# Another order for the scan and for the passage behind it, and a gate mix on VectorE, in a gated recurrent layer with a feed-forward layer

## The reference

```python
u = x @ W_in + b_in
g = sigmoid(x @ W_gate + b_gate)
def step(h_prev, (u_t, g_t, x_t)):
    h_t = tanh(h_prev @ A + u_t @ Bm)
    y_t = h_t @ C.T + u_t @ D.T
    y_t = g_t * y_t + (1.0 - g_t) * x_t        # the gate mix
ys = scan(step, h0 = 0)
x1 = layernorm(x + (ys @ W_out + b_out + x))
h = gelu(x1 @ binarize(w1).T + b1)             # 1024 hidden features
out = layernorm(x1 + h @ binarize(w2).T + b2)
```

## Time and profile before

| | us |
|---|---|
| median of 3 runs (lowest, highest) | 444.82 (444.19, 445.14) |
| the profiled execution | 445.74 |
| its span | 443.9 |
| PE busy | 416.0 (94% of the span) |
| DVE busy | 365.7 (82%) |
| ACT busy | 321.9 (73%) |
| POOL busy | 304.9 (69%) |

### The profile page before, as it was taken

One profiled execution on the slowest core, in us unless ns is written; L12 is line 12 of the kernel. 1 busy time (PEld: TensorE's weight loads), 2 busy tenths in 40 slices (PEclk: granted clock), 3 DMA queues, 4 the chain that ended last, 5 costly groups with the idle time before them and its releaser, 6 DMA issues.

```text
span 443.9 us, 7765 instructions
## 1 busy us (share of the span) xinstructions
PE 416.0 (94%) x2699; PEld 309.2 (70%) x2699; DVE 365.7 (82%) x778; ACT 321.9 (73%) x604; POOL 304.9 (69%) x322
## 2 busy tenths in 40 slices
PE   7999999988876999999999999999999999999882
PEld 5899887876733676776767767677676776766651
DVE  2787778856054889999999999999999999998584
ACT  1346765645264769798898988989889899797791
POOL 6465663253349896977979779797797977683523
PEclk9999999999896999999999999999999999999998
DMA  7954360001010112124241442313423134231222
GB/s 223 362 170 120 121 141 1 0 1 35 15 49 0 49 47 49 48 49 120 71 96 50 95 124 67 96 54 90 128 63 96 63 81 133 58 97 45 52 96 95
DMA packets 43896, 37.19 MB, mean 84 GB/s; under 512 B 35504, under 2 KB 37296, under 8 KB 43856
## 3 DMA queue, kind: packets, MB, share of 16 engines
q1 hardware_dynamic: 42528, 35.66, 28.1%
q0 software_dynamic: 272, 0.66, 0.5%
q10 hardware_dynamic: 1056, 0.36, 0.3%
HBM read 19.90 MB, written 8.39 MB: 64 GB/s over the span
## 4 chain that ended last, share of the span: by engine, by line
PE 58%; DVE 24%; POOL 6%; issue 5%; ACT 5%; ACTq 0%; POOLq 0%; DVEq 0%
PE bank L1089 16%; PE bank L1077 14%; PE bank L939 10%; DVE hid L1443 7%; PE bank L907 6%; PE bank L918 3%; ACT hid L700 3%; POOL xg_lo L433 3%; DVE gT L1456 3%; PE bank L856 3%; DVE bank L1428 3%; DVE bank L1449 2%; DVE xT L1188 2%; PE bank L849 2%; DVE gT L1438 2%
## 5 line engine op out<-in xcount | busy, mean ns | idle before, releaser
L1077 PE MATMUL bank<-xT,w1s 128*128 128x512 f16 x512 | 128.6, 384 | 2.4 <-DVE hid L1443 1.7
L1089 PE MATMUL bank<-w2s,hid 128*128 128x256 f16 x1024 | 125.3, 273 | 1.7 <-DVE gT L1456 0.8
L1089 PEld LDWEIGHTS bank<-w2s,hid 128*128 128x128 f16 x1024 | 98.5, 98 | 32.6 <-issue 5.6
L692 ACT ACTIVATE bank<-bank,b_col,alpha 128x512 f32<-128x512 f32 x128 | 96.7, 756 | 22.2 <-PE bank L1077 21.9
L1443 DVE SCALAR_TENSOR_TENSOR hid<-bank,small,hid 128x512 f16<-128x512 f32 x128 | 95.2, 745 | 14.7 <-ACT hid L700 14.7
L700 ACT ACTIVATE hid<-bank,small 128x512 f16<-128x512 f32 x128 | 86.5, 691 | 19.0 <-PE bank L1089 17.8
L1077 PEld LDWEIGHTS bank<-xT,w1s 128*128 128x128 f16 x512 | 46.4, 99 | 49.6 <-DVE hid L1443 6.9
L639 ACT ACTIVATE hu<-bank 64x128 f32<-64x128 f32 x103 | 27.8, 270 | 52.8 <-PE bank L856 50.0
L453 POOL TENSOR_TENSOR ys_lo<-gT,ys_hi 128x512 fp32r<-128x512 f32 x30 | 38.2, 1277 | 24.9 <-ACT ys_hi L665 24.8
L448 POOL TENSOR_TENSOR gT<-gT,xT 128x512 f32<-128x512 f32 x30 | 38.2, 1274 | 13.0 <-DVE gT L1327 12.8
L440 POOL TENSOR_TENSOR hu_lo<-hu,hu_hi 64x512 fp32r<-64x512 f32 x30 | 37.9, 1262 | 13.2 <-ACT hu_hi L687 10.9
(11 more groups left out here) (159 smaller groups left out, 823.7 us busy)
## 6 DMA issues: line engine op xcount, KB each, us to landing
x_load<-in_L_attn_x SPq DMA_DIRECT2D x16, 512.0 KB, 3.4
gT<-in_L_attn_x SPq DMA_DIRECT2D x15, 512.0 KB, 3.8
out_rows<-gT SPq DMA_DIRECT2D x15, 512.0 KB, 3.5
gT<-in_L_ffn_w SPq DMA_DIRECT2D x2, 1024.0 KB, 7.6
gT<-in_L_attn_x SPq DMA_DIRECT2D x4, 128.0 KB, 2.6
out_rows<-gT SPq DMA_DIRECT2D x2, 256.0 KB, 2.0
xT<-gT SPq DMA_TRANSPOSE x28, 3.2
w_gate<-in_L_attn_W_gate ACTq DMA_DIRECT2D x1, 256.0 KB, 6.9
```

What stands on the lines that cost most here:

```text
L692: nc.scalar.activation(bank[which][:, :], bank[which][:, :], ACT.Gelu, bias=b1_col[:, c:c + 1], scale=alpha1[:, c:c + 1]).then_inc(s_gelu, 1)
L1077: done = nc.tensor.matmul(bank[which][:, :], w1s[:, c, k, :], x1T[:, n, :, part, :, k, :], start=(k == 0 and part == 0), stop=(k == KD - 1 ...
L1089: done = nc.tensor.matmul(bank[tile // 2][:, tile % 2 * DM:(tile % 2 + 1) * DM], hid[:, c % 3, part, tile * P:(tile + 1) * P], w2s[:, :, c ...
```

## The change

No operation on data changes but one: the gate mix of blocks 1 and 2. Everything else is the order in which instructions stand, and the waits that follow from it.

1. **Scan.** The transposes of every block come one step earlier (turned_at, and one extra in the opening), and from block 3 on DVE writes x_out of the second half ahead of u_out of the block before. prepare_rows moves from step 80 to step 76 (PREP, its last matmul to step 79). The y products of block 0 move from steps 86 and 90 to 83 and 85 (FIRST_Y). first_y_high (the high part of the states for them) moves on DVE from behind gate_x_hi(11) to just behind the second weight reduction, hu_low(0, 0) and hu_low(0, 1) on POOL from behind gate_x_low(10) to behind gate_x_low(6). gate_x_lo(9) goes behind the splitting of the C/D table; gate_x_hi(13) and gate_x_lo(13) behind block 0's mix.
2. **Passage.** The orders on PE, DVE, ACT and POOL from step 103 to iteration(1) are new. PE takes the flag's matmul ahead of gate_half(14, 0), and y(1, 0) and y(1, 1) ahead of gate_half(15, 1). ACT's switch to the Gelu table comes later.
3. **Gate mix of blocks 1 and 2.** less_x, then early_gate leaves the product in the bank and early_mix on DVE adds x out of the bank into SBUF; POOL's mix of these blocks is gone, four instructions. The products y(2, 0), y(2, 1), y(3, 0) and hidden(0, 0) now wait for the mix (s_ys), not for the gate alone, since the bank is read by it.
4. **End.** ffn_out(14, 5) stands ahead of hidden(15, 0) and ffn_out(14, 6) ahead of hidden(15, 1); ACT puts the block-12 second norms between the hidden chunks 0 to 3 of block 15; DVE interleaves ffn_scale and second_sum of block 14; the last moments come ahead of a wait.

The diff, cut to its core:

```diff
-    PREP = 10
+    PREP = 9
...
-    FIRST_Y = (WARM + 11 * STEPS + 2, WARM + 12 * STEPS + 2)
+    FIRST_Y = (WARM + 10 * STEPS + 3, WARM + 11 * STEPS + 1)
...
-        return divmod(t + 2 * STEPS, STEPS)
+        return divmod(t + 2 * STEPS + 1, STEPS)
...
-            for place in (6, 8, 10):
-                gate_x_low(place)
-            pool.wait_ge(s_xgl[0], 6)
+            gate_x_low(6)
+            pool.wait_ge(s_xgl[0], 2)
             hu_low(0, 0)
             hu_low(0, 1)
-            gate_x_low(12)
+            for place in (8, 10, 12):
+                gate_x_low(place)
             ys_low(0, 0)
             ys_low(0, 1)
             pool.wait_ge(s_const, 3)
@@ -532,26 +532,20 @@
             add_bias(0)
             pool.wait_ge(s_xb, 1)
             hu_low(1, 0)
+            hu_low(1, 1)
             first_rstd(0, 0)
-            pool.wait_ge(s_rs1, 1)
-            hu_low(1, 1)
             first_rstd(0, 1)
-            mix(1, 0)
-            pool.wait_ge(s_ys, KD + 1)
+            pool.wait_ge(s_rs1, 2)
             hu_low(2, 0)
-            mix(1, 1)
-            pool.wait_ge(s_ys, KD + 2)
             hu_low(2, 1)
+            add_bias(1)
             ys_low(1, 0)
             ys_low(1, 1)
-            add_bias(1)
             residual(0)
-            mix(2, 0)
-            first_rstd(1, 0)
-            pool.wait_ge(s_rs1, 3)
+            pool.wait_ge(s_x1b, 1)
             hu_low(3, 0)
             hu_low(3, 1)
-            mix(2, 1)
+            first_rstd(1, 0)
             first_rstd(1, 1)
             ys_low(2, 0)
             ys_low(2, 1)
@@ -757,22 +751,21 @@
...
-            gate(14, 0)
             act.wait_ge(s_done, 1)
             hu_high(1, 0)
+            gate(14, 0)
             hu_high(1, 1)
             gate(14, 1)
             gate(15, 0)
+            hu_high(2, 0)
+            hu_high(2, 1)
+            x1_hi(0, 0)
+            x1_hi(0, 1)
+            ys_high(1, 0)
             gate(15, 1)
+            ys_high(1, 1)
             nc.scalar.activation(small[0:1, 29:30], ident[0:1, 0:1], ACT.Gelu)
             act.wait_ge(s_scale, 1)
...
-                if n > 1 or (n == 1 and m == 0):
+                if n == 2 and m == 0:
+                    pe.wait_ge(s_ys, KD + 1)
+                elif (n, m) in ((2, 1), (3, 0)):
+                    pe.wait_ge(s_ys, n * KD + m)
+                elif n > 1:
                     pe.wait_ge(s_t, n * KD + m)
...
                     u_whole(2, 1)
+                    transpose_step(*turned_at(t))
...
-                    if o + 2 < NB:
-                        transpose_step(o + 2, s)
+                    if turned_at(t)[0] < NB:
+                        transpose_step(*turned_at(t))
...
                 gate_piece(i)
-            gate_half(14, 0)
             pe.wait_ge(s_cmp, 3)
             nc.tensor.matmul(bank[2][0:1, 0:1], gap_flag, ones[0:NS, 0:1], start=True, stop=True).then_inc(s_cnt, 1)
-            gate_half(14, 1)
+            gate_half(14, 0)
             pe.wait_ge(s_flag, 1)
...
-                    pe.wait_ge(s_t, 2 * KD)
+                    pe.wait_ge(s_ys, 2 * KD)
...
+            gate_half(14, 1)
             gate_half(15, 0)
-            gate_half(15, 1)
             y_products(1, 0)
             y_products(1, 1)
+            gate_half(15, 1)
             x1_transposes(0, 0)
             x1_transposes(0, 1)
             y_products(2, 0)
             pe.wait_ge(s_wt, 32)
             pe.wait_ge(s_scale, 1)
-
-
             hidden(0, 0)
             hidden(0, 1)
+            hidden(0, 2)
             y_products(2, 1)
             out_products(1, 0)
             out_products(1, 1)
-            hidden(0, 2)
+            hidden(0, 3)
             ffn_out(0, 0)
-            hidden(0, 3)
+            hidden(0, 4)
             ffn_out(0, 1)
-            hidden(0, 4)
+            ffn_out(0, 2)
+            hidden(0, 5)
...
+            ffn_out(NB - 2, 5)
             hidden(NB - 1, 0)
-            ffn_out(NB - 2, 5)
+            ffn_out(NB - 2, 6)
             hidden(NB - 1, 1)
-            ffn_out(NB - 2, 6)
...
-            for o in range(2, NB - 1):
-                if o >= WHOLE_U:
-                    u_out(o, 1)
-                    x_out(o + 1, 1)
-                    x_high(o + 1, 1)
+            x_out(4, 0)
+            u_out(3, 0)
+            x_high(4, 0)
+            for o in range(WHOLE_U, NB - 1):
+                x_out(o + 1, 1)
+                u_out(o, 1)
+                x_high(o + 1, 1)
                 if o + 2 < NB:
                     x_out(o + 2, 0)
                 u_out(o + 1, 0)
                 if o + 2 < NB:
                     x_high(o + 2, 0)
...
+
+            def first_y_high(half):
+
+                dve.wait_ge(s_h, 1 + WARM + STEPS)
+                dve.wait_ge(s_sgn, 2)
+                nc.vector.tensor_copy(y0_hu_hi[HALVES[half], :, :], beside(0, half)).then_inc(s_huhi, 1)
+
+            dve.wait_ge(s_prep, 1)
+            first_y_high(0)
+            first_y_high(1)
             gate_x_hi(7)
             gate_x_lo(7)
+            gate_x_hi(8)
...
-            gate_x_lo(9)
-            gate_x_hi(10)
...
-            def first_y_high(half):
-
-                dve.wait_ge(s_h, 1 + WARM + STEPS)
-                dve.wait_ge(s_sgn, 2)
-                nc.vector.tensor_copy(y0_hu_hi[HALVES[half], :, :], beside(0, half)).then_inc(s_huhi, 1)
-
-            gate_x_hi(11)
-            first_y_high(0)
-            first_y_high(1)
-            gate_x_lo(11)
+            gate_x_lo(9)
+            gate_x_hi(10)
...
+            def early_gate(n, m):
+
+                dve.wait_ge(s_yd, n * KD + m + 1)
+                nc.vector.tensor_tensor(y_bank(n, m)[:, :], y_bank(n, m)[:, :], gT[:, n, m, :], ALU.mult).then_inc(s_t, 1)
+
+            def early_mix(n, m):
+                dve.wait_ge(s_t, n * KD + m + 1)
+                nc.vector.tensor_tensor(gT[:, n, m, :], y_bank(n, m)[:, :], xT[:, n, m, :], ALU.add).then_inc(s_ys, 1)
+
...
             first_moments(0, 1)
+            first_norm(0, 0)
             less_x(1, 0)
-            gate_y(1, 0)
-            first_norm(0, 0)
+            less_x(1, 1)
+            early_gate(1, 0)
             first_norm(0, 1)
-            less_x(1, 1)
-            gate_y(1, 1)
+            early_mix(1, 0)
+            early_gate(1, 1)
             x1_lo(0, 0)
+            early_mix(1, 1)
             x1_lo(0, 1)
             less_x(2, 0)
-            gate_y(2, 0)
+            early_gate(2, 0)
...
+            last_moments(1)
             dve.wait_ge(s_last_root, 1)
             nc.vector.scalar_tensor_tensor(out=shift2[:, NB - 1, 0:2], in0=moments[:, 1, 0:2, 0], scalar=-1.0,
                                            in1=rstd2[:, NB - 1, 0:2], op0=ALU.mult, op1=ALU.mult).then_inc(s_last_shift, 1)
-            last_moments(1)
```

More of the change, by code:

```diff
@@ L81, in pieces_at @@
             return 0
-        return 1 if turned_at(t)[0] < NB + 1 and t < NB * STEPS - 7 else 2 if t < NB * STEPS - STEPS else 3
+        return 1 if t < NB * STEPS - 7 else 2 if t < NB * STEPS - STEPS else 3
     def pieces_before(t):
@@ L799, in _ @@
                 hidden_hi(NB - 2, c)
-            for c in range(2):
-                hidden_gelu(NB - 1, c)
-                hidden_hi(NB - 1, c)
+            hidden_gelu(NB - 1, 0)
+            second_norm(NB - 4, 1)
+            hidden_hi(NB - 1, 0)
+            hidden_gelu(NB - 1, 1)
+            second_norm(NB - 4, 2)
+            hidden_hi(NB - 1, 1)
             hidden_gelu(NB - 1, 2)
-            second_norm(NB - 4, 1)
             hidden_hi(NB - 1, 2)
             hidden_gelu(NB - 1, 3)
-            second_norm(NB - 4, 2)
-            hidden_gelu(NB - 1, 4)
+            hidden_hi(NB - 1, 3)
             second_norm(NB - 4, 3)
-            for c in range(3, 5):
-                hidden_hi(NB - 1, c)
-            for c in range(5, HC):
+            for c in range(4, HC):
                 hidden_gelu(NB - 1, c)
@@ L1251, in _ @@
             gate_x_hi(5)
+            gate_x_lo(5)
             u_out(NB - 1, 1)
-            gate_x_lo(5)
             dve.wait_ge(s_w12, 32)
@@ L1270, in _ @@
             nc.vector.memset(ones, 1.0)
-            gate_x_hi(8)
             dve.wait_ge(s_const, 3)
@@ L1317, in _ @@
             nc.vector.tensor_scalar(alpha2_row[:, :], bank[3][:, 0:DM], inv_scale, None, ALU.mult).then_inc(s_prep, 1)
-            gate_x_hi(12)
+            gate_x_hi(11)
+            gate_x_lo(11)
             def less_x(n, m):
@@ L1344, in _ @@
             less_x(0, 0)
+            less_x(0, 1)
+            first_gate(0)
+            first_gate(1)
+            first_mix(0)
+            gate_x_hi(12)
+            first_mix(1)
+            first_high(0)
+            first_high(1)
             gate_x_hi(13)
-            first_gate(0)
             gate_x_lo(13)
-            first_mix(0)
-            less_x(0, 1)
-            first_gate(1)
-            first_high(0)
-            first_mix(1)
-            first_high(1)
             dve.wait_ge(s_h, 1 + WARM + L)
@@ L1527, in _ @@
```

(26 more changed lines are left out.)

33 lines of the change are left out of this document (8 added, 25 removed).

## The result

The changed kernel takes 424.4 us (median of 4 runs, 423.89 to 425.9), the kernel before 444.82. The ratio is 0.9548 (95% interval 0.9522 to 0.9574). The profiled execution of the changed kernel took 424.39, its span is 422.5, 21.4 shorter than before. The forecast was 425.5, a gain of 19.3; measured are 20.4 by the medians.

A forecast was written before the change was run, and what follows sets the result against it. PE bounds the loop, busy 39.89 of 40 us; only scan, passage and end can move. 445.74 − 11.7 − 6.3 − 1.4 = 426.3, less 0.9 for the median 425.4, written 425.5; range 422 to 431.5.

The forecast's parts named there:

- First half: Scan, steps 12 to 59: the copy leaves the closed turn, which falls from 4.04 to 3.67; 5.0 us gained.
- Second half: Scan, steps 59 to 103: three PE stalls go, 7.8 us gained, and new waits cost 1.1.
- the bound's matmul: Second half of the scan: its PE stall of 0.36 us goes through PREP and its later step.
- gate_x_lo(9) come 0.3 late: Step 79 of the scan: gate_x_lo(9), behind the C/D table and the bound, is 0.3 us late (0 to 0.8).
- The new wait at step 71: Scan: gate_x_lo(7) is ready 0.8 us after the gate piece at step 71 wants it (0 to 1.7).
- the case for which the prediction had 1.7: Step 71: upper bound of gate_x_lo(7)'s lateness, 1.7 us, if both instructions of the pair collide.
- Passage: Step 103 to iteration 1: 34.4 us instead of 40.7, 6.3 gained; first hidden product 4.3 earlier.
- a wait in front of y(3, 0): Passage, behind the first hidden product: PE waits 0.7 us for the mix.
- End: End of the kernel: 1.0 us from PE waits of 0.89 and 0.84, 0.4 from last_moments(1); 1.4 together.
- The turn in the scan: Rival, chance 0.12: the scan's turn stays bound, the 5.0 us are lost, 430.5 us.
- The passage gave nothing back: Rival, chance 0.15: the passage gives its gain back, by low clock 2.5 and waits 1.5; 429.5 us.
- The low clock: Rival, chance 0.02: pauses keep PE at 1.2 GHz through the scan, each fall costing 1.8 to 2.5; 447 us or more.

The follow-up runs named there:

- the two single experiments: Kernel before with only the transposes one step earlier (444.98 us), and with only DVE's x_out copy ahead of u_out (442.33 us).
- the first half alone: Kernel before with every transpose one step earlier and DVE's x_out copy ahead of u_out, nothing else: 440.19 us.
- mix on POOL: Changed kernel with the gate mix of blocks 1 and 2 back on POOL, all else as changed: 430.76 us.
- longer pause: Changed kernel with one more DVE instruction, an unused maximum over 128x2048 of x, ahead of the second x1_lo: 428.37 us.
- the two tries and both: Changed kernel with gate_x_hi(7), gate_x_lo(7) ahead of first_y_high (424.01 us); with POOL's first_rstd(0, 0) ahead of hu_low(1, 1) (424.4); with both edits (424.66).
- The second half alone: Kernel before with only PREP, FIRST_Y, first_y_high, hu_low, the C/D table and block 0's mix order changed: 438.42 us.

## Why the prediction was right

**First half.** The turn closed through u_out and the copy as read from the earlier trace rows. Both parts are needed, as the two single experiments show. Forecast 5.0, the first half alone 4.8. Between steps 12 and 59 it is 4.6 in the trace. The missing 0.4 is step 15, which takes 1.32 instead of 0.92 because the transposes, now a step earlier, stand there waiting for the DMA of x (the row at 24.96 above). That wait stands in three of the eight traces with the early transposes (1.68 in the first half alone, 1.42 with the transposes alone) and in none of the six without. The five others (mix on POOL, longer pause, the two tries and both) take 43.2 us from step 12 to 59, a gain of 5.0. The prediction named the shorter lead of this DMA, but gave it no price. The 0.6 ahead of step 12 is no clear part of the gain: step 12 stood at 21.2 to 22.0 in traces that share this code.

**Second half.** The waits of 1.53 and 3.85 and the low clock went. Two small terms were wrong and cancelled by luck: I let the bound's matmul stop waiting (0.36) and gate_x_lo(9) come 0.3 late. Neither happened; step 79 is 0.39 longer than a plain one, as step 82 was before. The new wait at step 71 was put at 0.8; the step takes 1.88, 0.96 more than a plain one. This is nearer than the reasoning deserved: it took only one of DVE's two instructions to be lengthened by POOL, and both were, the case for which the prediction had 1.7. The second half alone shows that case, with 1.60 more; in the changed kernel the first half brings DVE there 0.63 earlier. 6.5 measured, 6.7 forecast.

**Passage.** The first hidden product came at +14.9, forecast 15.4. DVE's row of instructions is what sets it, as forecast; its last five took 3.1 us instead of 3.5. Behind it I had put 18.3 of products and 0.7 of a wait in front of y(3, 0). The wait does not exist, and the products took 17.75. This is the one term that was mis-sized by more than 1 us: 3.2 gained for 2.0. Part of the 3.2 belongs to the trace that it is taken against: in three of the five other traces of the old order it took 0.7 to 1.3 less. The clock did not fall at the pauses of 0.87 and 1.56; the longer pause shows that it does at 3.8, and what it costs there is 1.8, where the prediction had 2.5.

**End.** 1.6 by the traces, 2.15 alone by the medians, 1.4 forecast.

**The rivals.** The turn in the scan did not stay bound; it would have with either of the two parts left out. The passage gave nothing back on DVE, though DVE is what PE waits for there. The low clock was the right thing to fear, but it did not come before the last matmul: no pause of PE in the changed trace is longer than 1.56.

The terms missed by +0.2 (with the start counted), −0.2, +1.8 and +0.2 us, together 1.9 by the profiled executions (424.39 against 426.3) and 1.1 by the medians. That the total is nearer by the medians is luck in part: the 0.9 that the profiled execution of the kernel before took above its median was taken off the forecast too, while that of the changed kernel is at its median.

## What to carry to other kernels

Follow a periodic wait once round all the engines and add up what stands in the ring; an instruction of 0.69 that belongs to the next block but is queued inside the ring costs its time every turn, and taking it out pays only if its own input is there early enough. An engine that does two kinds of work in turn for a waiting one (mix, low part, mix, low part) is the place to look in a start-up: moving the 1.3 us instructions to an engine that does them in 0.69 out of the bank gave three quarters of the passage's gain by the traces, more than a third of it by sparing PE the low clock. A pause costs more than its length when PE's clock falls with it, so the longest one is worth the most. And since one execution pays more for the low clock than another, a gain read from two traces can be off by more than a microsecond: the passage gave 8.1 by the traces and 6.5 by the medians.
